# Token stage of a small vision transformer in two halves of 32 images on one Trainium2 core

## The chip, the cores and the metric

The kernel runs on one core of one Trainium2 chip. The metric is device time in microseconds (us) of one launch; smaller is better. TensorE (PE), VectorE (DVE), ScalarE (ACT) and GpSimd (POOL) compute; SyncE (SP) issues nearly all DMAs. Each engine works through its own instructions in order, and semaphores order the engines among each other.

## What is computed

```python
# 64 images of 3x96x96: 36 patches of 768 values each; D = 192, T = 37 tokens per image
x = layernorm(patches, ln1_g, ln1_b) @ W_lin + b_lin          # tokens [64, 36, 192]
x = layernorm(x, ln2_g, ln2_b)
h = concat([cls_token, x]) + pos_embedding                    # [64, 37, 192]
# attention, 8 heads, relative positions
q, k, v = LN(h) @ Wq, LN(h) @ Wk, LN(h) @ Wv
h = h + (softmax((q + rw) @ k.T + shift((q + rr) @ rk.T)) @ v) @ Wo + bo
h = h + moe(LN(h))                                            # 8 experts, top 2, capacity 740
```

## The kernel before

**Token stage.** The host lays the image out as x[6 patch rows][64 images][6 patches * 768]. On the chip a "unit" is 128 patches: partition p holds image p % 64 and patch row 2j + p // 64, and unit (j, w), j = 0..2 and w = 0..5, is the patch column w. So 18 units u = 6j + w cover all 64 images, and every image is complete only after the last of them. `load_x(j)` (L455) brings 2.36 MB in four DMAs of 64 partitions; s_x[j][f] covers the three units of one half f.

For each unit PE transposes six blocks (L645) and multiplies by the centred weights (L656), ACT copies the transposes out of PSUM (L1043), and DVE reads the product (L1312). DVE also takes the statistics of the unit six later (L1267), and after every third unit the statistics of the second layernorm (L1292 to L1297); POOL turns variances into 1/sigma (L1708). DVE normalises three units at a time (`ln2_rows`, L1303), and POOL multiplies by the gain and adds the positions (`finish`, L1738 and L1740); DVE does this itself for the last three units (L1329, L1330). PE may be four products ahead of DVE (four PSUM banks, s_tze).

**Round trip.** SP stores each finished three units into the DRAM tensor h_tokens, image by image (L509). Then it waits for all stores (L527) and reads the rows back as 22 groups of 111 rows, three images each (`h_all`, L531 and L532): first groups 0 and 1, then the other 20.

**Attention.** It takes two groups per step, 11 steps. Step s on PE: projections for queries and keys (L697), relative scores (L705), values (L741), transposes of the rows of step s + 1 (L688), content scores (L749), between the later parts of step s - 1. The relative scores make a round trip through DRAM of their own (`rel_roundtrip`: stores L545, reads with a skewed pitch L553), and DVE's softmax of step s (L1377 to L1384) waits for it; it stands in DVE's program of step s + 1. The q, k and v weights lie as `wraw` over the first x pieces in the tensor `wide`, so they are loaded (L524) once nine units are transposed; ACT rounds them to `wh` (L1120) and DVE forms the remainder `wl` (L1335, L1336). DVE prepares the rows of step 0 in `ln1_var` (L1343 to L1345), `ln1_rows` (L1351) and `rows_low` (L1358, L1359).

**Order on SP.** Token weights, load_x(0), load_x(1), seven constant tables (block, ind, pos_f, iota8, eidx, upper, real), g2B, b2B, six posB, two clsB, load_x(2), seven attention weights with wo (0.59 MB), zeros into `sums` (0.59 MB), the stores of j = 0, cls and pad rows, twelve DMAs of Wq, Wk and Wv, the other stores, the reads of h_all, then rel_roundtrip(0).

Of the kernel before, what the change touches and what calls it, by code (L numbers as in the profile page):

```python
# [51 lines left out]
N_EARLY, N_CONST, N_QKV, N_AW = 5, 17, 12, 7  # L52
# [46 lines left out]
def build(nc, x, ln1_g, ln1_b, W_lin, b_lin, ln2_g, ln2_b, pos_embedding, cls_token,  # L99
# [7 lines left out]
    with ExitStack() as ctx:  # L107
# [74 lines left out]
        piece = carve(wide)  # L182
        qw = piece(128, HB * G2).rearrange("p (m n) -> p m n", m=HB)
# [93 lines left out]
        posB = piece(128, NH * NH // 2 * D).rearrange("p (j n) -> p j n", j=NH // 2)  # L277
# [69 lines left out]
        s_ho = [sem(f"tok_rows_stored{j}") for j in range(NH // 2)]  # L347
# [106 lines left out]
        def _(sp):  # L454
            def load_x(j):  # L455

                for f in range(2):
                    for u in range(2):
                        sp.dma_start(wide[64 * u:64 * u + 64, j * XF + f * (XF // 2):j * XF + (f + 1) * (XF // 2)],
                                     x[2 * j + u][:, f * (XF // 2):(f + 1) * (XF // 2)]).then_inc(s_x[j][f], 16)  # L460
# [9 lines left out]
            sp.dma_start(block[:, :], c_block).then_inc(s_const, 16)  # L470
            sp.dma_start(ind[:, :], c_ind).then_inc(s_const, 16)
            sp.dma_start(pos_f[:, :], c_pos).then_inc(s_const, 16)  # L472
            sp.dma_start(iota8[:, :, :], c_iota[0:G]).then_inc(s_const, 16)
            sp.dma_start(eidx[:, :], c_iota[:, 0, :]).then_inc(s_const, 16)
            sp.dma_start(upper[:, :], c_upper).then_inc(s_const, 16)
            sp.dma_start(real[:, :], c_real).then_inc(s_const, 16)
            sp.dma_start(g2B[:, :], bc(row(ln2_g), [128, D])).then_inc(s_const, 16)
            sp.dma_start(b2B[:, :], bc(row(ln2_b), [128, D])).then_inc(s_const, 16)
            for n in range(NH):
                src = pos_embedding[0, 1 + n * NH:1 + (n + 1) * NH, :].rearrange("(a t) d -> a (t d)", a=1)  # L480
                sp.dma_start(posB[64 * (n % 2):64 * (n % 2) + 64, n // 2, :],
                             bc(src, [64, NH * D])).then_inc(s_const, 16)
# [6 lines left out]
            sp.dma_start(wo[:, :, :], Wo.rearrange("(c p) d -> p c d", p=128)).then_inc(s_aw, 16)  # L489
# [10 lines left out]
            hv = h_dram[0:B * T, :].rearrange("(b t) d -> b t d", t=T)  # L500
            for j in range(NH // 2):
                for f in range(2):
                    if (j, f) == (NH // 2 - 1, 1):
                        sp.wait_ge(s_ht_last, 1)
                    else:
                        sp.wait_ge(s_ht, 2 * j + f + 1)
                    for u in range(2):
                        t0 = 1 + (2 * j + u) * NH + f * NF
                        sp.dma_start(hv[:, t0:t0 + NF, :].rearrange("b t d -> b (t d)"),  # L509
                                     zt[64 * u:64 * u + 64, j, f * NF:(f + 1) * NF].rearrange("p t d -> p (t d)")  # L510
                                     ).then_inc(s_ho[j], 16)
                if j == 0:
                    sp.wait_ge(s_cls, 1)
                    sp.dma_start(hv[:, 0, :], clsP[:, :]).then_inc(s_ho[0], 16)
                    sp.dma_start(h_dram[B * T:ROWS, :], zeros[0:ROWS - B * T, 0:D]).then_inc(s_ho[0], 16)


                    sp.wait_ge(s_tT, 3 * NH // 2)
                    sp.wait_ge(s_v1, 2)
                    at = 0  # L520
                    for W in (Wq, Wk, Wv):
                        n = W.shape[1]
                        for p0, b_, r0, rows_ in ((0, 0, 0, 128), (0, 1, 0, 64), (64, 1, 128, 64), (0, 2, 64, 128)):
                            sp.dma_start(wraw[p0:p0 + rows_, b_, at:at + n], W[r0:r0 + rows_]).then_inc(s_qkv, 16)  # L524
                        at += n
            for j in range(NH // 2):
                sp.wait_ge(s_ho[j], 96 if j == 0 else 64)  # L527

            hg = h_dram.rearrange("(g p) d -> p g d", p=G)
            for a, b_ in ((0, 2), (2, NG)):  # L530
                sp.dma_start(h_all[0:SPLIT, a:b_], hg[0:SPLIT, a:b_]).then_inc(s_h, 16)  # L531
                sp.dma_start(h_all[SPLIT:G, a:b_], hg[SPLIT:G, a:b_]).then_inc(s_h, 16)  # L532
                sp.wait_ge(s_h, 32 if a == 0 else 64)
# [92 lines left out]
        def _(pe):  # L626
# [42 lines left out]


            pe.wait_ge(s_tze, UNITS)
            pe.wait_ge(s_const, 16 * N_CONST)
            pe.wait_ge(s_aw, 16 * N_AW)
            for m in range(HB):
                last = pe.matmul(PS[:, 6, m * R:(m + 1) * R], wrk[:, m * 128:(m + 1) * 128], pos_f[:, :],
                                 start=(m == 0), stop=(m == HB - 1), skip_group_check=True)
            last.then_inc(s_rkp, 1)

# [100 lines left out]
            def step(s):  # L779
# [42 lines left out]
                pe.wait_ge(s_re[1], s + 1)  # L822
                values(0)
# [72 lines left out]
            pe.wait_ge(s_wh, 1)  # L896
            pe.wait_ge(s_wl, 1)
# [140 lines left out]
        def _(act):  # L1038
            for u in range(UNITS):
                act.wait_ge(s_tT, u + 1)  # L1040
                if u >= 2:
                    act.wait_ge(s_tz, u - 1)
                nc.scalar.copy(xTt[:, u % 2, :, :].rearrange("p (a c) n -> p a (c n)", a=2),  # L1043
                               PS[:, 2 * (u % 2):2 * (u % 2) + 2, 0:384]).then_inc(s_tTa, 1)

# [177 lines left out]
        def _(dve):  # L1223
            v = nc.vector

            def ch(ins):

                dve.drain()
# [33 lines left out]
            def ln1_stats(j, w):  # L1262

                if w % (NH // 2) == 0:
                    dve.wait_ge(s_x[j][w // (NH // 2)], 32)
# [40 lines left out]

            for j in range(NH // 2):
                dve.wait_ge(s_r1, j + 1)
                for w in range(NH):
                    u = j * NH + w  # L1310
                    dve.wait_ge(s_tz, u + 1)
                    v.scalar_tensor_tensor(zt[:, j, w, :], PS[:, 4 + u % 4, 0:D], rs1[:, j, w:w + 1], cB[:, :],  # L1312
                                           ALU.mult, ALU.add).then_inc(s_tze, 1)

                    if j + 1 < NH // 2:
                        ln1_stats(j + 1, w)
                        if w == NH - 1:
                            ln1_end(j + 1)
                    if w % NF == NF - 1:
                        ln2_stats(j, w // NF)  # L1320
                    if w % NF == 1 and u >= NF:
                        ln2_rows((u - NF) // NH, (u - NF) // NF % 2)
            ln2_rows(NH // 2 - 1, 1)

            dve.wait_ge(s_pos, NH // 2)
            dve.wait_ge(s_tn, NH)
            z3 = zt[:, NH // 2 - 1, NF:]
            three = lambda b_: bc(b_[:, :].rearrange("p (a d) -> p a d", a=1), [128, NF, D])
            ch(v.tensor_tensor(z3, z3, three(g2B), ALU.mult))  # L1329
            v.tensor_tensor(z3, z3, posB[:, NH // 2 - 1, NF * D:].rearrange("p (w d) -> p w d", w=NF),  # L1330
                            ALU.add).then_inc(s_ht_last, 1)
            dve.wait_ge(s_const, 16 * N_CONST)

            dve.wait_ge(s_wh, 1)
            v.tensor_tensor(wl[:, 0, :], wraw[:, 0, :], wh[:, 0, :].bitcast(F32), ALU.subtract)  # L1335
# [579 lines left out]
```

## Time and profile before

| | |
|---|---|
| median of 3 runs | 622.51 us (621.87 to 623.0) |
| profiled execution, whole | 623.27 us |
| its span, first to last instruction | 621.5 us |
| PE busy | 87% of the span |
| DVE busy | 69% |
| last token product ends | 67.5 us |
| first projection of the attention | 90.08 us |
| first softmax instruction of step 0 | 106.80 us |

The profile is one execution; its spans and starts are in us from the first instruction. What lies around the span is 1.8 us. A group's idle time names what released the engine. The granted clock of PE is 1.00 at 2.4 GHz and 0.50 at 1.2 GHz.

### The profile page before, as it was taken

Reading aid. Unit: us, or ns where it says so; the run is one execution under the profiler, and the core shown is the slowest. Engines: PE = TensorE matmul, PEld = TensorE weight load, DVE = VectorE, ACT = ScalarE, POOL = GpSimd, SP = SyncE. Lnnn points to the kernel's source line nnn. Section 1 sums busy time; section 2 is a strip of 40 time slices with the busy share of each in tenths; the row PEclk is TensorE's granted clock in tenths of the full one; section 3 lists DMA queues with packets and bytes.
Section 4 is the critical chain, followed back from the end, with each engine's and each line's share of the span. In section 5 each row is a group of like instructions: output and inputs, shape, how many; then the busy total and the mean of one; then the engine's idle time right before and its main releaser. Section 6 shows DMA issues by size and latency. Waiting matters only on the chain.

```text
span 621.5 us, 12359 instructions
## 1 busy us (share of the span) xinstructions
PE 539.1 (87%) x4284; PEld 501.0 (81%) x4284; DVE 431.6 (69%) x1002; ACT 258.7 (42%) x412; POOL 222.0 (36%) x206
## 2 busy tenths in 40 slices
PE   5989428999999999999999796667999999999982
PEld 4988428989999899899899683344899999999982
DVE  6828764776776777777767757672778777777753
ACT  1322403542443434425425204402865685595560
POOL 0137711012021021120120205017587788776463
PEclk9998759999999999999999857869999999999997
DMA  8799663202102112012022008504275476476160
GB/s 200 166 223 225 196 132 60 51 2 51 40 11 50 28 22 50 17 34 50 6 45 44 8 1 219 150 1 133 81 164 134 94 165 139 93 144 150 19 166 30
DMA packets 61497, 55.84 MB, mean 90 GB/s; under 512 B 28693, under 2 KB 52053, under 8 KB 60671
## 3 DMA queue, kind: packets, MB, share of 16 engines
q1 hardware_dynamic: 52319, 46.92, 30.4%
q0 software_dynamic: 9152, 8.59, 8.4%
q8 instruction: 14, 0.23, 0.2%
q14 instruction: 12, 0.10, 0.1%
HBM read 40.21 MB, written 18.27 MB: 94 GB/s over the span
## 4 chain that ended last, share of the span: by engine, by line
PE 45%; DVE 14%; ACT 13%; issue 10%; SPq 5%; DMA 5%; POOL 4%; DVEq 2%; POOLq 1%; ACTq 0%
PE PS L1018 7%; PE PS L741 6%; PE PS L718 6%; PE PS L697 5%; ACT wide L1055 4%; PE PS L1016 4%; ACT hTh L1197 3%; DMA wide<-x 2%; PE PS L734 2%; PE PS L732 2%; PE PS L733 2%; PE PS L725 2%; DVE hTl L1657 2%; PE PS L993 2%; SPq L472 2%
## 5 line engine op out<-in xcount | busy, mean ns | idle before, releaser
L1708 POOL TENSOR_TENSOR rs<-ve,nhalf 111x1 f32<-111x1 f32 (+2 forms) x37 | 24.5, 662 | 270.0 <-DVE ve L1345 195.0
L1839 POOL DMA_INDIRECT running_sums<-ye,gid x42 | 74.8, 1780 | 33.5 <-DVE ye L1681 24.3
L1018 PE MATMUL PS<-w2hl,hTh 128*128 128x384 f32 (+1 forms) x288 | 82.8, 357 | 0.0
L1016 PE MATMUL PS<-w2hl,hTl 128*128 128x192 f32 (+1 forms) x288 | 73.6, 255 | 4.2 <-DVE hTl L1657 4.0
L1813 POOL DMA_INDIRECT xe<-routed_rows,gid x48 | 53.1, 1107 | 42.8 <-DVE gid L1622 28.6
L993 PE MATMUL PS<-xeT,w1h 128*128 128x370 f32 x288 | 64.2, 331 | 2.1 <-issue 1.4
L1657 DVE TENSOR_TENSOR hTl<-hf,hTh 128x740 fp32r<-128x740 f32 x48 | 44.6, 929 | 24.6 <-ACT hTh L1197 23.1
L1016 PEld LDWEIGHTS PS<-w2hl,hTl 128*128 128x128 f32 (+1 forms) x288 | 53.7, 186 | 6.8 <-issue 5.6
L1018 PEld LDWEIGHTS PS<-w2hl,hTh 128*128 128x128 f32 (+1 forms) x288 | 52.9, 184 | 0.5
L993 PEld LDWEIGHTS PS<-xeT,w1h 128*128 128x128 f32 x288 | 50.4, 188 | 2.8 <-issue 1.8
L697 PE MATMUL PS<-xT,wh 128*128 128x222 f32 x264 | 47.3, 289 | 5.5 <-DVE xT L1359 5.5
L993 PE MATMUL PS<-xeT,w1l 128*128 128x370 f32 x192 | 48.0, 331 | 0.0
L1194 ACT ACTIVATE hf<-PS,b1s 128x740 f32<-128x740 f32 x48 | 42.1, 877 | 6.3 <-PE PS L993 3.9
L697 PEld LDWEIGHTS PS<-xT,wh 128*128 128x128 f32 x264 | 38.2, 199 | 7.9 <-issue 7.8
L656 PE MATMUL PS<-narrow 128*128 128x192 f32 x216 | 38.8, 331 | 0.0
L718 PE MATMUL PS<-wide 111*111 111x96 f32 x336 | 36.9, 270 | 1.0 <-DVE wide L1498 1.0
L718 PEld LDWEIGHTS PS<-wide 111*111 111x111 f32 x336 | 35.0, 183 | 1.9 <-DVE wide L1498 1.1
L1377 DVE SCALAR_TENSOR_TENSOR wide<-PS,ind,wide 111x296 f32<-111x296 f32 x64 | 33.6, 524 | 4.1
L656 PEld LDWEIGHTS PS<-narrow 128*128 128x128 f32 x216 | 35.5, 194 | 0.5 <-issue 0.5
L697 PE MATMUL PS<-xT,wl 128*128 128x222 f32 x176 | 34.9, 281 | 0.0
L1043 ACT COPY narrow<-PS 128x768 f32<-128x768 f32 x18 | 14.4, 799 | 47.8 <-PE PS L645 47.8
L732 PE MATMUL PS<-woh,oTh 128*111 128x192 f32 x126 | 33.5, 266 | 0.9 <-DVE oTl L1407 0.9
(240 smaller groups left out, 1286.1 us busy)
## 6 DMA issues: line engine op xcount, KB each, us to landing
wide<-x SPq DMA_DIRECT2D x12, 576.0 KB, 13.7
w1r<-L_ffn_W SPq DMA_DIRECT2D x16, 384.0 KB, 4.8
rel_scores<-wide SPq DMA_DIRECT2D x66, 73.0 KB
w2r<-L_ffn_W SPq DMA_DIRECT2D x8, 576.0 KB, 4.4
w1r<-L_ffn_W SPq DMA_DIRECT2D x16, 192.0 KB, 4.5
wide<-rel_scores SPq DMA_DIRECT2D x22, 111.0 KB, 2.3
out<-running_sums SPq DMA_DIRECT2D x1, 1776.0 KB, 8.0
narrow<-L_tok_pos_embedding SPq DMA_DIRECT2D x6, 288.0 KB
```

The lines of the kernel that those rows point to most:

```text
L656: last = pe.matmul(PS[:, 4 + u % 4, 0:D], xTt[:, u % 2, c, :], W_cen[:, c, :], start=(c == 0), stop=(c == PC - 1))
L697: last = pe.matmul(PS[:, bank, (m % 2) * G2:(m % 2 + 1) * G2], lhsT, xT[:, b_, :], start=(nth == 0 and m % 2 == 0), stop=(nth == len(BLOCK ...
L718: last = pe.matmul(heads(4 - 2 * g, V)[:, j, :], pT[:, g, j * G:(j + 1) * G], v_sb[:, g, h * V:(h + 1) * V], start=(j % HB == 0), stop=Tru ...
L732: pe.matmul(PS[0:G, g, 0:D], oTh[:, g, at], woh[:, c, :], start=(c == 0), stop=False)
L741: last = pe.matmul(PS[0:G, 2 * g + n, 0:HB * V], xT[:, b_, g * G:(g + 1) * G], (wh, wl)[w][:, b_, at:at + HB * V], start=(nth == 0), stop= ...
L993: last = pe.matmul(PS[:, hidden_bank(c) + n, 0:HALF], (w1h, w1l)[hl][:, b_, w], xeT[:, b_, n * HALF:(n + 1) * HALF], start=(nth == 0), sto ...
L1016: pe.matmul(PS[0:n, bank, 0:D], hTl[:, c, at], w2hl[:, c, 0, :], start=(c == 0), stop=False, skip_group_check=True)
L1018: last = pe.matmul(PS[0:n, bank, 0:2 * D], hTh[:, c, at], both(w2hl[:, c, :, :]), start=False, stop=(c == HC - 1), skip_group_check=True)
L1194: last = nc.scalar.activation(hf[:, c % 2, :].rearrange("p (a n) -> p a n", a=2), src, ACT.Gelu, bias=b1s[:, p, c:c + 1])
L1657: v.tensor_tensor(hTl[:, c, :], hf[:, c % 2, :], hTh[:, c, :].bitcast(F32), ALU.subtract).then_inc(s_hl, 1)
L1813: p_.indirect_dma_start(xe[0:r, p, n, :], None, xr_dram, bass.IndirectOffsetOnAxis(ap=gid[0:r, e, n:n + 1], axis=0), bounds_check=B * T - ...
L1839: p_.indirect_dma_start(sums, at, ye[0:r, e % 2, n, :], None, bounds_check=B * T + NT * 128 - 1, oob_is_err=True, compute_op=ALU.add).then ...
```

## The change

A unit is still 128 patches, but partition p now holds one of 32 images and one of four patch groups (patch row 2(q % 3) + u, left or right three columns), as `patches(q)` says. Chunk q = 0..5 is three units; chunks 0 to 2 (units 0 to 8) are all patches of images 0 to 31, chunks 3 to 5 those of images 32 to 63. x, posB and the stores go in DMAs of 32 partitions; posB needs half its bytes, since both halves use the same. After chunk 2 the rows of the first 32 images are stored and groups 0 to 9 are read; the other twelve groups are read after the last store. DVE's first attention work stands behind units 15, 16 and 17; the weights are rounded in four pieces of columns. wo and the zeros of `sums` are issued behind the first read, and the constant tables behind all of x.

```diff
-N_EARLY, N_CONST, N_QKV, N_AW = 5, 17, 12, 7
+N_EARLY, N_CONST, N_QKV, N_AW = 5, 16, 12, 14
+CHUNKS = NH
+HALF_B = B // 2
+QKV_PIECES = ((0, 512), (512, 1024), (1024, 1408), (1408, 1792))
+GROUPS_A = 10
...
+            def patches(q):
+                for u in range(2):
+                    for h in range(2):
+                        yield 32 * (2 * u + h), 2 * (q % (CHUNKS // 2)) + u, NF * h
+
+            def load_x(q):
+                images = slice(q // (CHUNKS // 2) * HALF_B, (q // (CHUNKS // 2) + 1) * HALF_B)
+                for p0, n, w in patches(q):
+                    sp.dma_start(wide[p0:p0 + HALF_B, q * (XF // 2):(q + 1) * (XF // 2)],
+                                 x[n][images, w * PD:(w + NF) * PD]).then_inc(s_x[q // 2][q % 2], 16)
...
             load_x(0)
             load_x(1)
-            sp.dma_start(block[:, :], c_block).then_inc(s_const, 16)
...
+            load_x(2)
             sp.dma_start(g2B[:, :], bc(row(ln2_g), [128, D])).then_inc(s_const, 16)
...
+            for q in range(CHUNKS // 2):
+                for p0, n, w in patches(q):
+                    src = pos_embedding[0, 1 + n * NH + w:1 + n * NH + w + NF, :].rearrange("(a t) d -> a (t d)", a=1)
+                    sp.dma_start(posB[p0:p0 + HALF_B, q, :], bc(src, [HALF_B, NF * D])).then_inc(s_const, 16)
...
-            load_x(2)
+            load_x(3)
+            load_x(4)
+            load_x(5)
+            sp.dma_start(block[:, :], c_block).then_inc(s_aw, 16)
...
-            sp.dma_start(wo[:, :, :], Wo.rearrange("(c p) d -> p c d", p=128)).then_inc(s_aw, 16)
...
+            def load_rows(a, z):
+                sp.dma_start(h_all[0:SPLIT, a:z], hg[0:SPLIT, a:z]).then_inc(s_h, 16)
+                sp.dma_start(h_all[SPLIT:G, a:z], hg[SPLIT:G, a:z]).then_inc(s_h, 16)
+
+            sp.wait_ge(s_tT, 3 * NH // 2)
+            sp.wait_ge(s_v1, 2)
...
+                    sp.dma_start(wraw[p0:p0 + rows_, b_, at:at + n], W[r0:r0 + rows_]).then_inc(s_qkv, 16)
...
+            sp.wait_ge(s_cls, 1)
...
+            for q in range(CHUNKS // 2):
+                sp.wait_ge(s_ht, q + 1)
+                store_rows(q)
+            sp.wait_ge(s_ho[0], 16 * (4 * CHUNKS // 2 + 2))
+            load_rows(0, GROUPS_A)
+            sp.wait_ge(s_h, 32)
+            sp.dma_start(wo[:, :, :], Wo.rearrange("(c p) d -> p c d", p=128)).then_inc(s_aw, 16)
             sp.dma_start(sums[B * T:B * T + NT * 128].rearrange("(p n) d -> p n d", p=128),
                          bc(zeros[:, :].rearrange("p (a d) -> p a d", a=1), [128, NT, D])).then_inc(s_h2, 16)
...
+            for q in range(CHUNKS // 2, CHUNKS - 1):
+                sp.wait_ge(s_ht, q + 1)
+                store_rows(q)
+            sp.wait_ge(s_ht_last, 1)
+            store_rows(CHUNKS - 1)
+            sp.wait_ge(s_ho[1], 16 * 4 * CHUNKS // 2)
+            load_rows(GROUPS_A, NG)
...
             rows_transposed(0)
-            pe.wait_ge(s_wh, 1)
-            pe.wait_ge(s_wl, 1)
+            pe.wait_ge(s_tze, UNITS - 3)
+            pe.wait_ge(s_aw, 16 * N_AW)
+            for m in range(HB):
+                last = pe.matmul(PS[:, 6, m * R:(m + 1) * R], wrk[:, m * 128:(m + 1) * 128], pos_f[:, :],
+                                 start=(m == 0), stop=(m == HB - 1), skip_group_check=True)
+            last.then_inc(s_rkp, 1)
+            pe.wait_ge(s_wh, 2)
+            pe.wait_ge(s_wl, 2)
             step(0)
...
+                if u >= UNITS - NF:
+                    if u == UNITS - NF:
+                        act.wait_ge(s_qkv, 16 * N_QKV)
+                    a, z = QKV_PIECES[u - (UNITS - NF)]
+                    nc.scalar.copy(wh[:, :, a:z], wraw[:, :, a:z]).then_inc(s_wh, 1)
...
+                    if u == UNITS - 3:
+                        dve.wait_ge(s_h, 32)
+                        ln1_var(0)
+                    if u == UNITS - 2:
+                        ln1_rows(0)
+                        qkv_low(0)
+                    if u == UNITS - 1:
+                        qkv_low(1)
             rows_low(0)
+            dve.wait_ge(s_rkp, 1)
+            v.tensor_copy(rk[:, :, :].rearrange("p m r -> p (m r)"), PS[:, 6, 0:HB * R]).then_inc(s_rk, 1)
+            qkv_low(2)
+            qkv_low(3)
+            ln2_rows(NH // 2 - 1, 1)
+            dve.wait_ge(s_pos, NH // 2)
+            dve.wait_ge(s_tn, NH)
...
+                            ALU.add).then_inc(s_ht_last, 1)
+            dve.wait_ge(s_aw, 16 * N_AW)
             dve.wait_ge(s_woh, 1)
             v.tensor_tensor(wol[:, :, :], wo[:, :, :], woh[:, :, :].bitcast(F32), ALU.subtract).then_inc(s_wol, 1)
+            step(0)
             dve.wait_ge(s_h, 64)
-            dve.wait_ge(s_aw, 16 * N_AW)
...
-            step(0)
             step(1)
...
+            rstd1(2)
+            rstd2(1, 1)
+            finish(3)
+            rstd2(2, 0)
             ln1(0)
+            finish(4)
+            rstd2(2, 1)
+            pool.wait_ge(s_aw, 16 * N_AW)
```

In this order the pieces are: constants, SP, PE, ACT's loop over the units, DVE, and the end of POOL's token work. `store_rows(q)` issues four DMAs of 32 partitions, `qkv_low(n)` forms `wl` for the columns of piece n. Pieces of `wide` that the attention uses have other places. Nothing behind step 1 of the attention has other instructions.

## Rows read from the trace of the kernel before

**Rows 1.** Head of the page: the span.

```profile
span 621.5 us, 12359 instructions
```

**Rows 2.** PE's timeline: start us, us, line, operation, count [idle before it <-releaser].

```profile
47.87 1.54 PE L645 MATMUL PS<-ident,wide 128*128 128x128 f32 x6 [3.22 <-DMA wide<-x]
...
63.33 4.14 PE L656 MATMUL PS<-narrow 128*128 128x192 f32 x24
...
90.08 0.95 PE L697 MATMUL PS<-xT,wh 128*128 128x222 f32 x3 [1.59 <-DVE xT L1359]
```

**Rows 3.** Chain that ended last, in order of time: start us, us, what.

```profile
78.00 0.77 DVE narrow L1330
...
79.29 2.46 DMA h_tokens<-narrow
...
82.23 2.08 DMA h_all<-h_tokens
84.33 0.36 DVE st L1343
...
106.03 0.39 DVE xT L1358
```

**Rows 4.** SP's timeline: start and length of groups of DMA issues.

```profile
9.04 12.01 SPq L472 DMA_DIRECT2D pos_f<-c_pos  x1
...
21.42 4.27 SPq L474 DMA_DIRECT2D eidx<-c_iota  x1
...
38.34 9.08 SPq L490 DMA_DIRECT2D boB<-L_attn_bo  x1
...
58.24 2.17 SPq L524 DMA_DIRECT2D wide<-L_attn_Wq  x4
...
103.33 2.02 SPq L553 DMA_DIRECT2D wide<-rel_scores  x4
```

**Rows 5.** Stretches: length; busy PE, PEld, DVE, ACT, POOL; PE clock, DMA share, GB/s.

```profile
20.00:25.00 5.00, 5.00 (x37) 4.96 (x36) 3.56 (x14) 1.38 (x3) 1.37 (x1) 1.00 1.00 218
25.00:30.00 5.00, 5.00 (x37) 4.96 (x36) 4.50 (x16) 1.38 (x3) 0.86 (x1) 1.00 0.42 84
60.00:65.00 5.00, 5.00 (x35) 4.81 (x34) 4.55 (x17) 1.60 (x2) 3.71 (x4) 1.00 0.93 287
90.00:95.00 5.00, 4.92 (x23) 4.95 (x24) 1.20 (x1) 0.79 (x2) 0.00 (x0) 0.50 0.96 157
```

**Rows 6.** Landing times of the twelve DMAs of L459 (x): us from issue.

```profile
DMA to landing us min/median/max: 5.7/13.7/20.1
```

**Rows 7.** DVE's timeline, columns as in Rows 2.

```profile
61.24 0.86 DVE L1292 BATCH_NORM_STATS2 bnt<-narrow 128x6 f32<-128x192 f32 x3
...
62.77 0.74 DVE L1312 SCALAR_TENSOR_TENSOR narrow<-PS,rs,cB 128x192 f32<-128x192 f32 x2
...
71.13 0.96 DVE L1303 TENSOR_SCALAR narrow<-narrow,mvt,rst 128x192 f32<-128x192 f32 x3 [2.75 <-POOL rst L1708]
...
78.68 2.02 DVE L1335 TENSOR_TENSOR wl<-wide,wh 128x1792 fp32r<-128x1792 f32 x1
...
86.76 0.67 DVE L1351 TENSOR_SCALAR xn<-h_all,mv,rs 111x192 f32<-111x192 f32 x2 [0.87 <-POOL rs L1708]
...
96.18 0.22 DVE L1543 CAST upperb<-upper 111x111 bf16<-111x111 f32 x1 [4.98 <-DMA h_all<-h_tokens]
...
106.80 1.72 DVE L1377 SCALAR_TENSOR_TENSOR wide<-PS,ind,wide 111x296 f32<-111x296 f32 x3
```

**Rows 8.** POOL's timeline, columns as in Rows 2.

```profile
64.76 1.41 POOL L1738 TENSOR_TENSOR narrow<-narrow,g2B 128x576 f32<-128x576 f32 x1 [1.08 <-DVE narrow L1303]
```

**Rows 9.** ACT's timeline, columns as in Rows 2.

```profile
71.27 4.67 ACT L1120 CAST wh<-wide 128x5376 fp32r<-128x5376 f32 x1 [7.06 <-DMA wide<-L_attn_Wv]
```

**Rows 10.** DMA issues by line up to 110 us: ns min/median/max, first and last start.

```profile
L509 SPq DMA_DIRECT2D h_tokens<-narrow x12: 446/597/1618, 53.4 to 79.3; - x12
...
L545 SPq DMA_DIRECT2D rel_scores<-wide x12: 314/319/339, 99.0 to 103.0; - x12
```

More of the change, by code:

```diff
@@ L346, in build @@
         s_cb = sem("bias_row_copied")
-        s_ho = [sem(f"tok_rows_stored{j}") for j in range(NH // 2)]
+        s_ho = [sem(f"tok_rows_stored{j}") for j in range(2)]
         s_h = sem("h_loaded")
@@ L526, in _ @@
[L526 to L533, printed above, removed]
+            for q in range(CHUNKS // 2, CHUNKS - 1):
+                sp.wait_ge(s_ht, q + 1)
+                store_rows(q)
@@ L668, in _ @@
                 tok_product(u)
[L671 to L677, printed above, removed]
             def rows_transposed(s):
@@ L822, in step @@
                 pe.wait_ge(s_re[1], s + 1)
+                if not before_:
+                    pe.wait_ge(s_wh, 4)
+                    pe.wait_ge(s_wl, 4)
                 values(0)
@@ L1305, in ln2_rows @@
                 last.then_inc(s_tn, 1)
[L1307 to L1335, printed above, removed]
-            v.tensor_tensor(wl[64:128, 1, :], wraw[64:128, 2, :], wh[64:128, 2, :].bitcast(F32),
-                            ALU.subtract).then_inc(s_wl, 1)
-            dve.wait_ge(s_rkp, 1)
-            v.tensor_copy(rk[:, :, :].rearrange("p m r -> p (m r)"), PS[:, 6, 0:HB * R]).then_inc(s_rk, 1)
             def ln1_var(s):
@@ L1533, in last_step, with qkv_low @@
                 repeat_prios(EARLY, NG)
-            dve.wait_ge(s_h, 32)
-            ln1_var(0)
-            ln1_rows(0)
-            rows_low(0)
+            def qkv_low(n):
+                dve.wait_ge(s_wh, n + 1)
+                a, z = QKV_PIECES[n]
+                v.tensor_tensor(wl[:, 0, a:z], wraw[:, 0, a:z], wh[:, 0, a:z].bitcast(F32), ALU.subtract)
+                v.tensor_tensor(wl[64:128, 1, a:z], wraw[64:128, 2, a:z], wh[64:128, 2, a:z].bitcast(F32),
+                                ALU.subtract).then_inc(s_wl, 1)
@@ new lines, in _ @@
+            for j in range(NH // 2):
+                dve.wait_ge(s_r1, j + 1)
+                for w in range(NH):
+                    u = j * NH + w
+                    dve.wait_ge(s_tz, u + 1)
+                    v.scalar_tensor_tensor(zt[:, j, w, :], PS[:, 4 + u % 4, 0:D], rs1[:, j, w:w + 1], cB[:, :],
+                                           ALU.mult, ALU.add).then_inc(s_tze, 1)
+                    if j + 1 < NH // 2:
+                        ln1_stats(j + 1, w)
+                        if w == NH - 1:
+                            ln1_end(j + 1)
+                    if w % NF == NF - 1:
+                        ln2_stats(j, w // NF)
+                    if w % NF == 1 and u >= NF:
+                        ln2_rows((u - NF) // NH, (u - NF) // NF % 2)
+                    if u == UNITS - 3:
[6 more added lines that the diff above has]
+                        qkv_low(1)
@@ new lines, in _ @@
+            rows_low(0)
+            dve.wait_ge(s_rkp, 1)
[5 more added lines that the diff above has]
+            dve.wait_ge(s_tn, NH)
+            z3 = zt[:, NH // 2 - 1, NF:]
+            three = lambda b_: bc(b_[:, :].rearrange("p (a d) -> p a d", a=1), [128, NF, D])
+            ch(v.tensor_tensor(z3, z3, three(g2B), ALU.mult))
```

137 lines of the change are left out of this document (58 added, 79 removed).

## Prediction

> **What bounds the kernel now.** I read the chain of work that ended last, in order of time, then the timelines of PE, DVE and SP side by side, then the stretches. PE's last token product ends at 67.5 (63.33 + 4.14) and its first projection starts at 90.08 [rows 2]: 22.6 us in which PE has 3 us of work. The chain shows why. The last three units are ready at 78.77, their store lands at 81.75, the first two groups are read by 84.31 [rows 3], DVE and POOL prepare them, and only then do the projections begin. From there one more latency chain leads to the first softmax instruction at 106.80 [rows 7], right behind the rows of step 1 at 106.03 [rows 3]; from then on PE is the bound and every step is the same in both kernels. So I take **the start of that softmax** as the point to move: whatever it gains, the span of 621.5 [rows 1] loses, and the time with it.
>
> Ahead of it lies the load of x. The eighth DMA was issued at 7.5 and landed at 27.6 (20.1 later, the longest [rows 6]); DMA was full at 218 GB/s from 20 to 25 and at 84 GB/s from 25 to 30 [rows 5], when SP was held in the issue of small tables (12.01 and 4.27 us [rows 4]). PE then waited 3.22 us for x at 47.87 [rows 2].
>
> **The change part by part.** I write H for the time when groups 0 to 9 have landed.
>
> *x and constants.* Of x 4.72 MB and 0.66 MB of weights had landed at 27.6. Now these bytes are chunks 0 to 2 (3.54 MB) plus g2B, b2B, cls (0.30) and the halved posB (0.88), in all the same 5.4 MB: chunk 2 at 22.3, constants at 27.6. Chunks 3, 4 and 5 follow at 1.18 MB / 218 GB/s [rows 5] = 5.4 us each: 33.0, 38.4, 43.8. Nothing small stands before them, so the weak stretch is not repeated here. The issue of 24 DMAs in place of 12 costs at most 12 x 0.6 = 7 us of SP and lies under the transfer (SP was up to 20 us ahead of the landing).
> In the x stretch 218 GB/s came from DMAs on 64 partitions, while the stretch with the weights, mostly on 128, shows 287 [rows 5]. The Trainium skill, "SBUF — State Buffer", section "Door 1: The DMA port swizzle", says that partitions 0 to 31 reach the same 8 ports as 0 to 63, 218 GB/s at best, and gives 189 against 196 GB/s for 1 MiB; the trace agrees with the first figure, and nothing in it shows 32 partitions on a load. An estimate from that page's two rates makes x 4% slower, 1.3 us, and the result later by that much.
>
> *DVE and POOL up to chunk 2.* DVE takes the statistics of unit 9 (chunk 3) while it evicts unit 3, so it now waits until 33.0 (before: 27.6). Per unit it needs 0.4 [rows 7] and about 1.0 us, per three units 1.5 for statistics (61.24 to 62.77) and 0.96 for the normalising [rows 7]; POOL needs 2 x 1.41 for `finish` [rows 8] and about 1 us for a root. Walked through, that gives 1/sigma of units 6 to 11 at 40, unit 8 at 46, its statistics at 47.7, `ln2_rows` of chunk 2 at 51.4 and its rows at 54.4. DVE reaches unit 15 at 60 and PE its last product at 63 to 66 (ACT waits behind unit 15 for the q, k, v weights; the four pieces of `wh` are the 4.67 us of [rows 9] cut up). All this lies before H and costs nothing.
>
> *SP.* Before, the small tables were accepted about when the x ahead of them landed: eidx at 25.7, the last at 27.4 against 27.6; boB at 47.4 [rows 4] against x at 47.8. So SP should have issued the seven tables at 43.8 and the six small weights by 47. It is then at the q, k, v weights: 3 x 2.2 us [rows 4] to 53.6, cls and pad rows to 54.6, twelve stores. A DMA of 32 partitions took 0.32 to issue, the stores of 64 0.60 [rows 10]; I take 0.35, so 58.8. The weights took 13.0 us from first issue to landing (58.24 to 71.27 [rows 4, 9]): 60. Behind them 0.88 MB of stores at 287 GB/s [rows 5], 3 us: stored at 63. Reading two groups took 2.5 us (81.84 to 84.31 [rows 3]), twenty 11.9 (84.33 to 96.18 [rows 7]); between them ten make 6.7. **H = 70.** If SP isn't held at all it still waits for the rows (54.4), stores to 55.8, + 2.5, at the earliest 58.3, + 6.7 = 65. If it is held once more as at eidx (4.27 us [rows 4]) and a store takes 0.60, H = 75. I take 70, since the holds have shown up twice.
>
> *DVE from H to the projections.* It stands at `s_h` behind unit 15; units 16 and 17 queue there, PE doesn't care. `ln1_var` 1.6 (84.33 to 85.89 [rows 3, 7]), evict 0.4, `ln2_rows` 1.0 (covers POOL's root), `ln1_rows` 0.7; wl piece 0 (2 x 2.02 x 512/1792 = 1.15 [rows 7]), evict 0.4, statistics 1.5, piece 1 1.15, `rows_low` 0.85: H + 8.8. PE begins at H + 9 = 79 in place of 90.08. wo is issued at H and PE waits for it ahead of wrk: 0.5 + 2 + 2 us plus 2.0 of products, H + 7 to 8, hidden, with 1 us to spare. PE has idled as before, so its clock will be 0.50 again as from 90 to 95 [rows 5]: nothing gained there.
>
> *The second half.* After `rows_low` come rk 0.5, wl pieces 2 and 3 1.7, `ln2_rows` 1.0, gain and positions 1.6 [rows 3]: H + 13.5. Four stores to issue 1.4 and landing 2.5 [rows 3]: H + 17.4. Twelve groups by the same two points 7.7: **H + 25**. This is the added wait: DVE's `s_h` at 64 stands ahead of softmax 0 and of everything behind it, and on SP the wait for the stores stands ahead of `rel_roundtrip(0)`. Its scores are ready at 79 + 8.8 and 10 = H + 18 and H + 19, SP comes to them at H + 19, its twelve stores take 4.3 us (twelve of 0.32 [rows 10] and gaps) and go through the same DMA engines behind the twelve groups: landed H + 25.5. Two reads 0.9 and 2.4: softmax may start at **H + 28.3**. Without that queueing it would be H + 27 (rows of step 1 at H + 25.8, then the six small instructions, 1.3, that were hidden before). I take the longer; both ends stay in the range.
>
> *Sum.* 106.8 - (70 + 28.3) = 8.5 us. Span 621.5 - 8.5 = 613.0; the profiled execution is 1.8 more, 614.8 against 623.3; the median of the runs, 622.5, gives **614.0**.
>
> **Rivals.**
> *Early.* SP runs ahead and only rows and DMA bound: H = 65, gain 13.5, 609.0. For it: the small tables no longer stand between parts of x. Against: boB was held 9.08 us [rows 4] just behind x.
> *Late SP.* H = 75, gain 3.5, 619.0.
> *The second half's tail is longer.* POOL's `finish(4)` stands behind `ln1(0)`, and DVE and POOL slow each other in places; 4 us more between H and softmax: 618.0. For it: DVE waited 2.75 us for POOL [rows 7] in just this place before.
> *It gives nothing.* Late SP and the long tail together: 622.5. The read of the second half merely takes the place of that of all rows.
> *Slower: the pieces of 32 partitions move more slowly.* 288 KB per DMA and two rows per engine. x is 7.08 MB, 32.5 us at 218 GB/s. All of the chain behind it, the q, k, v weights, the stores, H, shifts one for one, so it decides from 8.5 us, a rate 21% lower. At 148 GB/s (a read of h_all in short rows ran at 157 [rows 5]) it's 15.4 us: 622.5 + 6.9 = 629.4. Against: each row is still one run of 9,216 bytes.
> In the Trainium skill, "DMA: Bandwidth & Descriptors", section "Rules for kernel authors", 128 partitions and at least 1 MiB per DMA are asked for; this rule favours the rival, and no row here shows it for queued DMAs.
>
> **How the numbers follow.** Forecast 0.48 (610.5 to 617.5 by itself), early 0.17, late SP 0.13, long tail 0.08, nothing 0.04, slower 0.10. The range 608.5 to 621.0 leaves out the slower case, nothing, and a little of early. Faster by more than 0.2% (1.2 us, about what a measurement can tell): 0.48 + 0.17 + 0.13 + 0.08 = 0.86; same 0.04; slower 0.10.
>
> **What would show it.** x: PE's transposes of unit 12 without a wait, DMA near 220 GB/s until 43. SP: first q weight issued near 47 (40 early, 52 late). DVE: one long wait on h_all, from 60 to 70, ahead of `ln1_var(0)`. PE: first projection 9 us behind. A second wait on h_all at H + 25 or a wait of softmax on the skewed reads at H + 28. If the step from that softmax to the next isn't as long as before, my point for the sum is wrong; if x lands after 50, the slower rival holds.

## The result, and the profile after

The changed kernel takes 620.55 us (median of 13 runs, 618.09 to 622.56), the kernel before 622.65 us in the same comparison (13 runs, 621.83 to 624.57). The ratio is 0.9964, 95% interval 0.9953 to 0.9975: 2.1 us faster, where I had forecast 8.5. The time lies just inside my range of 608.5 to 621.0, but the upper end of that range stood for a late SP, which is not what happened. The profiled execution took 620.7 us.

Head of the page of the kernel after, and its slices of the granted clock:

```profile
span 618.9 us, 12396 instructions
...
PEclk9999788799999999999999757869999999999997
```

The span is 2.6 us shorter than in [rows 1]. In the first slices I look for the one weak place that I expected (the token stage's end) and see it drawn out: 7, 8, 8, 7, from the fifth slice to the eighth, 62 to 124 us.

SP's timeline after, the rows that answer to [rows 4]:

```profile
24.92 12.01 SPq L496 DMA_DIRECT2D pos_f<-c_pos  x1
...
37.55 4.35 SPq L498 DMA_DIRECT2D eidx<-c_iota  x1
...
45.90 2.13 SPq L530 DMA_DIRECT2D wide<-L_attn_Wq  x4
...
61.41 0.32 SPq L521 DMA_DIRECT2D h_all<-h_tokens  x1
...
87.80 0.32 SPq L521 DMA_DIRECT2D h_all<-h_tokens  x1
...
88.80 4.44 SPq L563 DMA_DIRECT2D rel_scores<-wide  x12
96.14 1.99 SPq L571 DMA_DIRECT2D wide<-rel_scores  x4
```

DVE's timeline after, answering to [rows 7] (the first row is the wait for chunk 3 of x, the second the one for groups 0 to 9):

```profile
34.46 1.02 DVE L1289 BATCH_NORM_STATS2 bn<-wide 128x6 f32<-128x384 f32 x2 [5.89 <-DMA wide<-x]
...
68.25 0.36 DVE L1331 BATCH_NORM_STATS2 st<-h_all 111x6 f32<-111x192 f32 x1 [5.07 <-DMA h_all<-h_tokens]
...
70.90 1.75 DVE L1339 TENSOR_SCALAR xn<-h_all,mv,rs 111x192 f32<-111x192 f32 x2
...
73.26 1.79 DVE L1528 TENSOR_TENSOR wl<-wide,wh 64x512 fp32r<-64x512 f32 x1
...
94.59 0.39 DVE L1346 TENSOR_TENSOR xT<-PS,xT 128x222 fp32r<-128x222 f32 x1 [4.84 <-ACT xT L1070]
...
98.75 1.74 DVE L1365 SCALAR_TENSOR_TENSOR wide<-PS,ind,wide 111x296 f32<-111x296 f32 x3 [2.07 <-DMA wide<-rel_scores]
...
128.19 1.73 DVE L1365 SCALAR_TENSOR_TENSOR wide<-PS,ind,wide 111x296 f32<-111x296 f32 x3
```

The row at 94.59 is the first of the transposed rows of step 1. The last two rows are the first instructions of the softmax of step 0 and of step 1. Up to the first of them the kernel gained 106.80 - 98.75 = 8.05 us. The same timeline of the kernel before has the softmax of step 1 here:

```profile
130.62 1.73 DVE L1377 SCALAR_TENSOR_TENSOR wide<-PS,ind,wide 111x296 f32<-111x296 f32 x3
```

So at the next softmax only 130.62 - 128.19 = 2.43 us are left. The step between them takes 29.44 us; before it took 23.82. From the softmax of step 1 to the end of the span it is 490.7 after and 490.9 before, so nothing that matters happens behind it. Of the 8.5 us that I forecast, 8.05 were there, and 5.6 of them were lost in one step of 11. It is what the prediction named as the sign that its point for the sum is wrong: the step from this softmax to the next isn't as long as before.

PE's timeline of the kernel after in this step:

```profile
79.37 0.95 PE L705 MATMUL PS<-xT,wh 128*128 128x222 f32 x3 [3.75 <-DVE xT L1347]
...
100.00 0.38 PE L705 MATMUL PS<-xT,wl 128*128 128x222 f32 x2
102.55 1.03 PE L720 MATMUL PS<-ident,wide 111*111 111x111 f32 x8 [2.16 <-ACT wide L1101]
103.90 1.77 PE L713 MATMUL PS<-rk,wide 64*111 64x73 f32 x16 [0.32 <-ACT wide L1077]
106.08 1.83 PE L720 MATMUL PS<-ident,wide 111*111 111x111 f32 x8 [0.41 <-ACT wide L1101]
107.84 1.78 PE L713 MATMUL PS<-rk,wide 64*111 64x73 f32 x16
109.54 6.29 PE L726 MATMUL PS<-wide 111*111 111x96 f32 x32
```

And of the kernel before:

```profile
111.45 0.39 PE L697 MATMUL PS<-xT,wl 128*128 128x222 f32 x2
111.67 0.94 PE L712 MATMUL PS<-ident,wide 111*111 111x111 f32 x8
112.54 1.00 PE L705 MATMUL PS<-rk,wide 64*111 64x73 f32 x16
114.13 1.03 PE L712 MATMUL PS<-ident,wide 111*111 111x111 f32 x8 [0.58 <-ACT wide L1079]
115.09 1.00 PE L705 MATMUL PS<-rk,wide 64*111 64x73 f32 x16
116.02 3.36 PE L718 MATMUL PS<-wide 111*111 111x96 f32 x32
```

The reader is to see two things. First, the way from the softmax of step 0 to the second batch of transposes is the same, 7.33 us: 98.75 to 106.08, and 106.80 to 114.13. The gaps of 2.16, 0.32 and 0.41 us cost nothing by themselves, since DVE and ACT set that pace. Second, from there on PE's products take up to twice as long: 1.83 in place of 1.03 for eight transposes, 6.29 in place of 3.36 for 32 products of probabilities and values. From the second batch of transposes to the softmax of step 1 it is 22.11 against 16.49, 5.62 more, which is all of it.

The stretches show what PE's clock did. Of the kernel after (columns as in [rows 5]):

```profile
100.00:105.00 5.00, 2.52 (x24) 2.16 (x24) 4.63 (x10) 3.45 (x9) 0.00 (x0) 0.85 0.00 0
105.00:110.00 5.00, 4.59 (x34) 4.06 (x33) 3.46 (x7) 1.91 (x4) 0.00 (x0) 0.50 0.21 54
110.00:115.00 5.00, 5.00 (x29) 5.00 (x28) 0.96 (x1) 0.30 (x1) 0.00 (x0) 0.50 0.29 67
115.00:120.00 5.00, 5.00 (x32) 4.94 (x32) 2.94 (x7) 1.83 (x3) 0.00 (x0) 0.78 0.24 39
```

And of the kernel before, the stretch with the same work:

```profile
110.00:115.00 5.00, 4.42 (x49) 4.15 (x47) 4.60 (x9) 4.61 (x11) 0.00 (x0) 1.00 0.00 0
```

The granted clock fell from 1.00 (2.4 GHz) to 0.50 (1.2 GHz) in the slice from 100 to 105, in which PE was busy for 2.52 of 5 us, and came back between 115 and 120. In the kernel before PE was busy for 4.42 of 5 us and kept 1.00. The timeline places the fall: the transposes at 102.55 still take 1.03 us, the next products at 103.90 take 1.77. The mean of 0.76 that the stretch from 103 to 104 has puts the fall at about 103.5, where the gap of 0.32 us begins. So of the three gaps only the first, of 2.16 us, lies clearly ahead of the fall, and the one of 0.41 us, at 105.67, lies behind it.

### The profile page after: what moved, and what is told of

Read it like the earlier page. It is cut to its first block, busy times and chain, and to the rows that moved or that the text cites. A ratio compares the mean times of both kernels' runs of the same rounds, so it can differ in the third digit from the quotient of the medians.

```text
span 618.9 us, 12396 instructions
## 1 busy us (share of the span) xinstructions
PE 542.4 (88%) x4284; PEld 503.6 (81%) x4284; DVE 433.4 (70%) x1008; ACT 258.8 (42%) x415; POOL 218.2 (35%) x206
## 4 chain that ended last, share of the span: by engine, by line
PE 44%; DVE 13%; ACT 12%; issue 10%; SPq 9%; DMA 5%; POOL 3%; DVEq 2%; POOLq 0%; ACTq 0%
PE PS L1035 7%; PE PS L726 6%; PE PS L749 6%; ACT wide L1077 4%; PE PS L705 4%; PE PS L1033 4%; ACT hTh L1219 3%; PE PS L733 2%; DVE hTl L1686 2%; PE PS L742 2%; PE PS L740 2%; PE PS L741 2%; PE PS L1010 2%; SPq L496 2%; ACT b2w L1225 2%
## 5 line engine op out<-in xcount | busy, mean ns | idle before, releaser
L1867 POOL DMA_INDIRECT running_sums<-ye,gid x42 | 73.4, 1747 | 34.8 <-DVE ye L1710 25.6
L726 PE MATMUL PS<-wide 111*111 111x96 f32 x336 | 39.8, 283 | 1.0 <-DVE wide L1486 1.0
L726 PEld LDWEIGHTS PS<-wide 111*111 111x111 f32 x336 | 37.9, 196 | 2.0 <-DVE wide L1486 1.1
L1090 ACT CAST oTh<-PS 128x666 fp32r<-128x666 f32 x21 | 15.1, 719 | 45.4 <-PE PS L733 45.4
```

Of the source, the lines that this page charges most:

```text
L726: last = pe.matmul(heads(4 - 2 * g, V)[:, j, :], pT[:, g, j * G:(j + 1) * G], v_sb[:, g, h * V:(h + 1) * V], start=(j % HB == 0), stop=Tru ...
L1867: p_.indirect_dma_start(sums, at, ye[0:r, e % 2, n, :], None, bounds_check=B * T + NT * 128 - 1, oob_is_err=True, compute_op=ALU.add).then ...
```

## The experiments

**Theory A**: PE idles around the softmax of step 0, loses its clock, and the slow products that follow take back 5 to 6 us. Before, PE was 5.0 us behind that softmax when it ended its projections of step 1 (111.84), now it is 1.6 (100.38), so it arrives at the transposes ahead of DVE and ACT. **Theory B**: the transfers. The stores of the relative scores queue behind the second read of rows, and steps 1 and 2 come too close behind them. By B the step gets shorter when the transfers come earlier, and stays long when PE alone is filled; by A when PE is kept busy, and the kernel before would lose the same time if its softmax came late.

In the added products PE multiplies a table of constants into a PSUM bank that is free at that moment; they do no useful work, and nothing of the computation is left out in any of the kernels. I read of each the step in two parts: softmax 0 to the second batch of transposes, and from there to softmax 1. The ratios are against the kernel before, on the same chip.

| | softmax 0 | to 2nd transposes | to softmax 1 | median | ratio, 95% |
|---|---|---|---|---|---|
| before | 106.80 | 7.33 | 16.49 | 622.65 | 1 |
| after | 98.75 | 7.33 | 22.11 | 620.55 | 0.9964 (0.9953 to 0.9975) |
| e1 after + 10 products | 98.97 | 7.34 | 21.73 | 615.69 | 0.9881 (0.9857 to 0.9905) |
| e8 after + 16 products | 97.71 | 7.33 | 16.91 | 616.52 | 0.9894 (0.9875 to 0.9912) |
| e2 order only | 95.79 | 7.34 | 21.65 | 618.37 | 0.9913 (0.9884 to 0.9943) |
| e5 order + 8 products | 98.24 | 7.33 | 16.95 | 614.25 | 0.9855 (0.9838 to 0.9873) |
| e3 before, softmax late | 111.16 | 7.33 | 21.12 | 632.72 | 1.0153 (1.0138 to 1.0167) |
| e7 e3 + 16 products | 112.16 | 7.33 | 21.34 | 632.37 | 1.0146 (1.0128 to 1.0164) |
| e9 e3 + 26 products | 110.53 | 7.33 | 16.55 | 628.18 | 1.0092 (1.0078 to 1.0105) |
| e4 order + earlier gaps filled | 95.04 | 7.34 | 21.72 | 617.84 | 0.9912 (0.9889 to 0.9934) |
| e6 e4 + 12 products | 95.76 | 7.79 | 16.95 | 612.76 | 0.9823 (0.9805 to 0.9841) |
| e10 e6, second gap longer filled | 94.18 | 7.80 | 16.95 | 612.20 | 0.9842 (0.9821 to 0.9864) |

Columns 2 to 4 are of one profiled execution each.

The last part of the step falls into two levels, 21.1 to 22.1 and 16.5 to 17.0 us. Within the lower one 0.4 us more stands in the kernels built on the kernel after (16.91 to 16.95 in e5, e6, e8, e10) than in those built on the kernel before (16.49, and 16.55 in e9). DVE stands for 0.47 us there ahead of an instruction (L1407 in the kernel after) without a wait that the profile shows, and not in the kernels built on the kernel before. What it is was not tested. So of the 5.62 us some 5.2 go with the clock, and 0.4 stay open.

**e1_pe_filled.** Ten products of 512 columns ahead of the key projections of step 1.

```diff
+                if is_step(s, 1):
+                    keep_warm(10, 3)
                 project(1, H * K, 3, s_kp)
```

> The changed kernel, plus ten products of 512 columns on PE in step 1, between the query and the key projections, where PE otherwise stands idle 2.2 us before softmax 0 is done. They do no useful work (their result is overwritten). Theory A (PE's clock): in the changed kernel softmax 0 began 8.05 us earlier than before, but PE's granted clock was 0.50 from about 103 to 117, right after that idle stretch, and that took 5.4 us back. With the stretch filled the clock stays at 1.00 and the span falls from 618.9 to 613.5-614.5. Theory B (the rest of the gain is lost to transfers: the second half's read, or the relative scores' round trip of step 1, end late): ten more products change nothing or cost up to 1 us: 618.5-620.

Measured: 615.69 us, 0.8% less than the kernel after, but the profiled execution was the slowest of the six (620.73 us, mean clock 0.937; the others 613.55 to 618.58 with 0.939 to 0.947). In it the first gap had shrunk from 2.16 to 0.35 us and the third had grown from 0.41 to 1.18; the clock fell all the same, and the step stayed at 29.07. Ten products (2.33 us) cut PE's idle time from 2.9 to 1.8 us and moved it back, which did not keep the clock.

**e8_pe_filled_more.** The same with 16.

```diff
+                if is_step(s, 1):
+                    keep_warm(16, 3)
                 project(1, H * K, 3, s_kp)
```

> The changed kernel with 16 products in place of ten ahead of the last key projection of step 1. Ten left the clock up in some executions only (613.6 to 616.4, clock 0.944-0.947, against 618.6 and 620.7, clock 0.937-0.939). Theory A: with 16 the gaps behind softmax 0 are closed too, and all executions are at 0.944 or more: 614-616, with a smaller spread. Theory B: each product costs its 0.2 us, 617-621 with the same spread.

PE's timeline of e8, then its stretches:

```profile
98.28 3.63 PE L784 MATMUL PS<-sums_to 128*128 128x512 bf16 x16
...
102.86 0.94 PE L720 MATMUL PS<-ident,wide 111*111 111x111 f32 x8
...
105.04 1.03 PE L720 MATMUL PS<-ident,wide 111*111 111x111 f32 x8 [0.31 <-ACT wide L1103]
106.00 1.00 PE L713 MATMUL PS<-rk,wide 64*111 64x73 f32 x16
106.94 3.36 PE L726 MATMUL PS<-wide 111*111 111x96 f32 x32
```

```profile
100.00:105.00 5.00, 4.73 (x43) 3.61 (x41) 4.72 (x9) 4.48 (x11) 0.00 (x0) 1.00 0.00 0
105.00:110.00 5.00, 4.96 (x55) 4.78 (x56) 3.38 (x7) 1.17 (x2) 0.00 (x0) 1.00 0.26 67
```

The same work, 3.6 us of useless products more, and the step takes 24.24 in place of 29.44 us: 5.2 back. The span of this execution is 612.8, close to my forecast of 613.0, and partly by luck: beside the 5.2 us it has a softmax 0 that began 1.0 us earlier (97.71 in place of 98.75). The transfers are those of the kernel after, so this is against theory B. The median, 616.52, keeps 4.4 of the 5.2 us against the kernel after by the two ratios (0.70% of 622.65). e1 and e8 can't be told apart by their medians.

**e2_rel_first.** SP sends the relative scores of step 0 ahead of the second read of rows, and DVE waits for those rows only behind step 1.

```diff
-            sp.wait_ge(s_ho[1], 16 * 4 * CHUNKS // 2)
-            load_rows(GROUPS_A, NG)
...
             rel_roundtrip(0)
+            sp.wait_ge(s_ho[1], 16 * 4 * CHUNKS // 2)
+            load_rows(GROUPS_A, NG)
...
             step(0)
-            dve.wait_ge(s_h, 64)
...
             step(1)
+            dve.wait_ge(s_h, 64)
```

> The changed kernel, with the read of groups 10 to 21 issued behind the relative scores' round trip of step 0 in place of ahead of it, and DVE's wait for these groups behind step 1 in place of behind step 0 (they are needed from step 4 on). Softmax 0 should begin 2 us earlier, near 96.7, bounded by the rows of step 1. Theory A (clock): PE's idle stretch before the softmax goes too, the clock stays up, and the span is 611-612.5. Theory B (transfers late): the gain is the 2 us alone, 616.5-617; if the later read collides with step 1's round trip, none.

Measured: SP began the stores of the scores at 86.44 in place of 88.80 and had issued the skewed reads by 92.80. Softmax 0 no longer waits for a DMA. Its distance from H (the landing of groups 0 to 9, 66.84 here) is 28.95 against 98.75 - 68.25 = 30.5: the queueing that I had priced at 1.3 us is worth 1.6. But the step stays at 28.99, and PE's timeline and stretches of e2 show the same fall of the clock with another pattern of gaps:

```profile
99.61 1.03 PE L720 MATMUL PS<-ident,wide 111*111 111x111 f32 x8 [0.26 <-ACT wide L1101]
100.95 1.00 PE L713 MATMUL PS<-rk,wide 64*111 64x73 f32 x16 [0.31 <-ACT wide L1077]
103.13 1.83 PE L720 MATMUL PS<-ident,wide 111*111 111x111 f32 x8 [1.17 <-ACT wide L1101]
```

```profile
100.00:105.00 5.00, 3.51 (x33) 3.00 (x31) 3.75 (x9) 3.61 (x9) 0.00 (x0) 0.79 0.07 15
105.00:110.00 5.00, 5.00 (x34) 4.87 (x35) 1.73 (x4) 0.65 (x1) 0.00 (x0) 0.50 0.30 75
```

Theory B falls: with the transfers of step 0 out of the way the step takes 28.99 in place of 29.44 us, and e8 shortened it without touching them. But A's forecast, a span of 611 to 612.5, was missed as well (615.8): the gaps changed their pattern and did not go, the clock fell, and only the earlier softmax was left. One of the seven runs took 612.49 us at a mean clock of 0.947, the others 616.76 to 619.81 at 0.936 to 0.939; it seems to have kept its clock, but it was not traced.

**e5_rel_first_filled.** e2 with eight products in step 1.

```diff
+                if is_step(s, 1):
+                    keep_warm(8, 3)
                 project(1, H * K, 3, s_kp)
```

> Round trip of step 0 ahead of the second read, DVE's wait behind step 1, and eight products without use on PE ahead of the last key projection of step 1. Theory A (PE's clock falls in step 1 because PE works with gaps there, and a fall costs about 5 us): nearly all executions now keep the clock through step 1 (mean granted clock 0.945 or more in place of 0.936-0.939), 611.5-613. Theory B (the time lost behind softmax 0 has another cause): 617-619, as without the products.

Measured: 614.25 us, all four runs within 0.8 us (613.72 to 614.56), step 24.28, clock 1.00 throughout it, one gap of 0.33 us left. Against e2, whose work it contains in full, it is 0.6% faster by the ratios, though in the profiled execution its H was late (69.71).

**e3_before_late_softmax.** The other direction: the kernel before, with nine small writes of zeros into unused rows ahead of softmax 0, which DVE does in 5.1 us.

```diff
+                if is_step(s, 1):
+                    for _ in range(9):
+                        ch(v.memset(h_all[:, NG:NG + 2, :], 0.0))
                 if before_:
                     softmax(s - 1)
```

> The kernel before, plus nine small memsets with drains on DVE (about 3.5-4 us) ahead of softmax 0, so that PE stands idle about 2.5 us in the same place as in the changed kernel. Theory A (clock): PE's clock falls to 0.50 behind this stretch and the span grows by far more than the delay, by 7-9 us, to 628.5-630.5. Theory B: it grows by the delay at most, 1-4 us, 622.5-625.5.

PE's timeline and stretches of e3:

```profile
114.96 1.83 PE L712 MATMUL PS<-ident,wide 111*111 111x111 f32 x8 [3.91 <-ACT wide L1079]
```

```profile
110.00:115.00 5.00, 1.09 (x11) 0.91 (x9) 4.22 (x9) 1.04 (x2) 0.00 (x0) 0.96 0.00 0
115.00:120.00 5.00, 5.00 (x32) 4.60 (x32) 4.07 (x8) 4.08 (x10) 0.00 (x0) 0.50 0.00 0
120.00:125.00 5.00, 5.00 (x34) 4.67 (x34) 1.65 (x3) 0.65 (x1) 0.00 (x0) 0.50 0.31 76
```

A delay of 5.1 us (4.4 at softmax 0 of the profiled execution) cost 9.9 us (632.72 against 622.85). The step has grown from 23.82 to 28.45 us without any change in its work. So a loss of this kind comes about without the 32-partition pieces, the two reads, or anything else that the change brings.

**e7_before_late_filled.** e3 with 16 products ahead of the key projections.

```diff
+                if is_step(s, 1):
+                    keep_warm(16, 3)
                 project(1, H * K, 3, s_kp)
```

> The kernel before with the same delay of 5.1 us ahead of softmax 0 as in the run with the late softmax (which cost 9.9 us), and 16 products without use on PE ahead of the last key projection of step 1, which fill 3.4 of the 3.9 us in which PE stood idle. Theory A: the clock does not fall, and only the delay is left: 4-5.5 us over before, 627-628.5. Theory B: no difference to the run without the products, 632-633.

A miss: 632.37 us, nothing gained. Its trace has gaps of 0.47, 0.32 and 1.18 us left between 115 and 119.5, the clock falls behind the last of them, and the step is 28.67. Either too few products, or theory A wrong.

```profile
115.96 1.03 PE L712 MATMUL PS<-ident,wide 111*111 111x111 f32 x8 [0.47 <-ACT wide L1081]
117.31 1.00 PE L705 MATMUL PS<-rk,wide 64*111 64x73 f32 x16 [0.32 <-ACT wide L1057]
119.49 1.83 PE L712 MATMUL PS<-ident,wide 111*111 111x111 f32 x8 [1.18 <-ACT wide L1081]
```

**e9_before_late_filled_more.** The same with 26 (5.79 us of products).

```diff
-                    keep_warm(16, 3)
+                    keep_warm(26, 3)
```

> The kernel before with the delay of 5.1 us ahead of softmax 0, and 26 products without use in place of 16. With 16 PE still stood idle for 0.47, 0.32 and 1.18 us between 115 and 119.5 and the clock fell at 119.7, and the time was that without products (632.4). With 26 PE comes to the first probabilities later than they do, as in the run with the round trip first and eight products. Theory A (the fall of the clock is the cost, and what sets it off is any sum of gaps here, not the one gap of 3.9 us): clock at 1.00 through step 1, only the delay is left, 627-628.5. Theory B (the delay costs twice its length for another reason): 632-634.

A stretch of e9 beside that of e3:

```profile
115.00:120.00 5.00, 4.88 (x60) 4.44 (x59) 4.59 (x9) 3.56 (x9) 0.00 (x0) 1.00 0.08 20
```

628.18 us, step 23.88, clock 1.00. Against the kernel before it is 0.92% slower, 5.7 us, close to the delay of 5.1 alone, and 0.61% faster than e3. It was a matter of how many products. The two runs together also separate the clock from the products themselves: 16 of them with the fallen clock gained nothing.

The profiled executions show how many are enough here. Where the clock stayed at 1.00 through the step (before, e5, e6, e8, e9, e10), PE ended its projections of step 1 between 5.0 and 6.2 us behind the start of softmax 0; where it fell (after, e1, e2, e3, e4, e7), between 0.1 us ahead of that start and 3.6 us behind it. Nothing was tried in between.

**e4_rel_first_warm_gap, e6_all, e10_all_more.** The earlier place where the clock is 0.50, ahead of the first projection. e4 is e2 with 30 products ahead of `rows_transposed(0)` and 14 behind the products of wrk; e6 adds 12 products in step 1; e10 is e6 with 22 in place of the 14.

```diff
+            keep_warm(30, 0)
             rows_transposed(0)
...
             last.then_inc(s_rkp, 1)
+            keep_warm(14, 0)
             pe.wait_ge(s_wh, 2)
```

> As the kernel with the round trip of step 0 ahead of the second read, plus products without use on PE in the two gaps of the transition: 30 between the last token product and the transposes of the rows of step 0, 14 behind the products of wrk. Theory A (clock): the first projections, 4 us of which ran at 0.50, run at 1.00 and end about 2 us earlier; the relative scores and softmax 0 follow, 609.5-611. Theory B: this part of PE's work is covered by DVE and SP, same as without the added products.

> As before with twelve products in step 1, and with the products in the two gaps of the transition as well (30 and 14). Theory A: clock at 1.00 from the token stage to the end of the attention, 610.5-612.5, the best of all. Theory B: 617-618.5.

> The best version (612.76) with 22 products in place of 14 in the second gap of the transition, where PE's clock still fell to 0.50 from about 79.5 to 83. Theory A: the first projections run at 1.00 throughout and end 1.5 us earlier; the relative scores and softmax 0 with them, 611-612. Theory B: another engine sets softmax 0, no difference, 612.3-613.2.

Measured: e4 is worth nothing beyond e2 (0.9912 and 0.9913), its clock falls in step 1 as in e2. e6 keeps the clock in step 1 and gives 612.76 us; a remainder of 0.50 from 79.5 to 83 was left. In e10 that is gone as well, by its stretch over the first projections:

```profile
75.00:80.00 5.00, 5.00 (x31) 2.99 (x29) 4.69 (x15) 0.49 (x2) 2.20 (x2) 1.00 0.16 39
```

Softmax 0 stands 26.84 behind H (67.34) in place of 28.44 in e6, and the profiled span is 609.4, but the median, 612.20, can't be told from that of e6. Twelve products in step 1 are a little too many: the first part of the step is 7.79 in place of 7.33. Both are faster than the kernel after by 1.2 to 1.4% and than the kernel before by 1.6 to 1.8%; they are the best that I have.

## Why the prediction was right and wrong

**x: right.** PE's transposes have no wait for x any more. DVE waited for chunk 3 until 34.46 (forecast 33.0), at 218 to 247 GB/s in every stretch from 5 to 40 us. Pieces of 32 partitions aren't slower than the 218 of [rows 5]; the slower rival falls. The estimate from the two rates of the Trainium skill, "SBUF — State Buffer", "Door 1: The DMA port swizzle", was 1.3 us later; chunk 3 was 1.5 later than my sum, though no stretch ran below the 218, so the trace gives no sign of the lower rate.

**SP: right.** `pos_f` held SP for 12.01 us again, in its new place, `eidx` 4.35 [rows 4]. The first q weight was issued at 45.90 (forecast 47), the twelve stores took 0.45 each, their data landed at 61.4 (63), and the read of ten groups took 6.8 us (6.7). H = 68.25 where I said 70 in a range of 65 to 75.

**From H to the projections: 2 us too short, and offset.** 11.1 us in place of 9. Two DVE instructions of this part took 1.75 and 1.79 us where their neighbours of the same shape took 0.67 and 0.69, while POOL ran `finish(4)` beside them. I had this in the rival with the long tail, not in the sum. PE's first projection: 79.37, forecast 79. Its clock was 0.50 there, as forecast.

**The second half and the queueing: right in kind, and in the total by luck.** Stores landed at 87.8 (87.4), relative scores behind the twelve groups at 96.1 (95.5), softmax 0 at 98.75 (98.3). The gain there is 8.05 us, forecast 8.5. But counted from H, softmax 0 came after 30.5 us and not 28.3, and most of these 2.2 us more are the 2 us of the part above. H was 1.75 us earlier than I had it, so the two errors cancel.

**The sum: wrong.** The step that failed is "from then on PE is the bound and every step is the same in both kernels", and with it the subtraction of the whole 8.5 us from the span. The instructions are the same and so is the way to the second batch of transposes (7.33 us in both), but the pace of PE behind it isn't. In the kernel before PE reached the transposes 5.0 us behind the start of the softmax, with 0.58 us of idle time up to the products of probabilities and values; the change took 8.05 us from the chain of the softmax and 11.46 (111.84 - 100.38) from PE, and nothing in the prediction asked for the second number. Of the 11.46, 10.71 are the earlier first projection (90.08 - 79.37), and most of the rest is the clock behind it, which came back after some 3.7 us in place of 5.2. The rows of step 1 moved with PE (94.59 in place of 106.03 [rows 3]). The softmax moved less, since two things now stand between these rows and it that PE does not wait for: the six small instructions of DVE, 1.3 us, and the wait of 2.07 us for the relative scores. I had priced both as a delay of the softmax, and not as a lead of PE. PE thus came 3.4 us nearer to the softmax and idled for 2.9 us in three pieces. Its clock fell at about the second of them, stayed at 0.50 for about 14 us, and the step gave 5.6 us back, 5.2 of them by the clock. 8.05 - 5.62 = 2.43, and the medians differ by 2.1. Filling the gaps brings it back (e8, e5, e6, e9), making them in the kernel before costs it (e3), moving the transfers leaves the step long (e2). Of the times that I gave for theory A ahead of the runs, those of e9 and, as a span, of e3 (629.8) were met. In e2, e4 and e7 the clock fell against my forecast and the time was missed by over 3 us; e5, e6, e8 and e10 came out 0.2 to 1.3 us above their ranges.

I had seen the clock at 0.50 in [rows 5] and asked what the change would do to that place; I hadn't asked it of a place where the clock was 1.00. None of the rivals was this one. "Late SP" (619.0) came nearest in time, for a reason that doesn't hold: SP was 1.1 us earlier than I had it.

**Open.** What makes single executions of e1 and e2 differ by 7 us: their mean clocks suggest that some keep the clock in step 1, but only one execution of each was traced. Nor was it tried whether fewer than eight products do in e5, or what the 0.47 us of DVE ahead of L1407 are.

## What to carry to other kernels

A chain that is shortened moves each engine by its own amount. For the engine that bounds the part behind, work out by how much it leads or trails its releaser after the change, and if it now arrives ahead of it, or much closer behind it than before, price the idle time and the clock behind it. Read the granted clock of the step behind the moved point before you carry a gain through to the end. Where PE must wait for a few us in a dense part, useless products in place of the wait were worth 0.6 to 0.9% here (e8, e5, e9 and e6 against the same kernels without them). Count them by the gaps of the trace: too few did nothing (e1's profiled execution, e7), and 12 in e6 made the first part of the step 0.46 us longer.

## What the runs showed of the hardware

Short idle times of PE among dense products came with a fall of the granted clock from 1.00 to 0.50 for 10 to 14 us: a gap of 2.16 us and the next of 0.32, at which it fell, in the kernel after; gaps of 0.26, 0.31 and 1.17 in e2 and of 0.47, 0.32 and 1.18 in e7, where it fell in the last; a single one of 3.91 in e3. With one gap of 0.3 to 0.6 us in the same place, or none, it stayed at 1.00 (before, e5, e8, e9). The sum of the gaps alone doesn't tell: in the kernel before gaps of 0.74 and 0.98 us, ahead of 100.11 and of 104.86, left the clock at 1.00. The Trainium skill, "TensorE: Matmul & The Clock Gate", section "A second HAM failure mode: psum-queue depth-cycling", tells of a kernel whose short idle times between groups of products cost it the clock; the traces of e2 and e7 agree.

Small tables issued behind queued loads of x held SP for 12.01 us (`pos_f`, in both kernels) and for 4.27 and 4.35 us (`eidx`), though they stood 16 us later in the second. `boB`, which held SP for 9.08 us close behind x in the kernel before [rows 4], took 0.31 us in the new place behind the other tables.
